# Rows gathered per block through a table made by one-hot matmuls, in place of scatters into slots: attention and mixture of experts on one core

## The reference

```
x = x + xattn(layernorm(x), ctx, ctx, mask, gamma, beta)
x = x + ffn(layernorm(x), w_gate, w_gate_up, w_down)

ffn: gate_probs = softmax(x @ w_gate); only the two highest per token stay, divided by their sum
     gu = einsum('bsd,edh->ebsh', x, w_gate_up);  g, u = split(gu, 2)
     expert_out = einsum('ebsf,efd->ebsd', silu(g) * u, w_down)
     out = einsum('bse,ebsd->bsd', gate_probs, expert_out)
```

## Time and profile before

| what | us |
|---|---|
| device time, median of 3 executions | 491.61 |
| lowest and highest of them | 488.97, 492.09 |
| profiled execution: its span, first to last instruction | 510.0 |
| PE busy in the span | 419.0 (82%) |
| DVE, ACT, POOL busy | 261.6, 201.6, 138.4 |
| TensorE's granted clock, tenths of full speed, in 40 slices of 12.75 us | `9975555575599999999999999999999999999996` |

### The profile page before, as it was taken

The page is one execution under the profiler, slowest core; times in us unless marked ns, Lnnn a source line. Parts: engine busy times, 40 slices in busy tenths (PEclk is TensorE's granted clock), DMA queues, the critical chain, the costliest instruction groups (busy, mean ns, idle before and its releaser), DMA issues.

```text
span 510.0 us, 10031 instructions
## 1 busy us (share of the span) xinstructions
PE 419.0 (82%) x2182; PEld 354.2 (69%) x2183; DVE 261.6 (51%) x601; ACT 201.6 (40%) x358; POOL 138.4 (27%) x122
## 2 busy tenths in 40 slices
PE   4979401060599999999999999999999999999990
PEld 3977201050488888888888888888888888888870
DVE  4786799320355465346556533555555347534330
ACT  2234557000345445345345333454454345423320
POOL 3393582777011211211211112112112112111121
PEclk9975555575599999999999999999999999999996
DMA  8559412642145164134425411354354115212101
GB/s 218 190 142 314 126 62 75 187 154 104 41 118 167 40 163 145 26 78 142 115 72 144 113 31 21 71 134 125 81 144 109 36 21 120 65 21 31 12 11 21
DMA packets 39105, 50.83 MB, mean 100 GB/s; under 512 B 5707, under 2 KB 33971, under 8 KB 39091
## 3 DMA queue, kind: packets, MB, share of 16 engines
q1 hardware_dynamic: 26323, 36.18, 22.9%
q0 software_dynamic: 7152, 9.34, 11.4%
q10 hardware_dynamic: 5616, 5.15, 3.8%
HBM read 33.95 MB, written 16.72 MB: 99 GB/s over the span
## 4 chain that ended last, share of the span: by engine, by line
PE 79%; DVE 6%; another core or an unknown queue 4%; DMA 4%; issue 2%; ACT 1%; POOL 1%; ACTq 1%; SPq 0%; POOLq 0%; DVEq 0%
PE bank L1289 41%; PE bank L1310 14%; PE bank L1312 7%; PE bank L1299 7%; PE bank L1210 3%; PE bank L1274 2%; PE bank L1191 2%; DMA ctx_sb<-in_ctx 1%; DVE act L592 1%; PE bank L1180 1%; DMA slots<-rows,idx 1%; DVE x_sb L648 1%; DVE stats L656 1%; DMA ctxT<-slots 1%
## 5 line engine op out<-in xcount | busy, mean ns | idle before, releaser
L1289 PE MATMUL bank<-w,tokT_hi 128*128 x624 | 173.9, 401 | 21.5 <-DVE tokT_lo L910 20.2
L539 POOL DMA_INDIRECT out<-y_sb,y_idx x39 | 61.4, 1575 | 311.5 <-DVE y_sb L935 300.8
L1289 PEld LDWEIGHTS bank<-w,tokT_hi 128*128 128x128 f32 x624 | 113.6, 191 | 43.9 <-issue 22.4
L919 DVE TENSOR_TENSOR act<-gated,bank 128x512 f32<-128x512 f32 x78 | 53.4, 685 | 137.3 <-ACT gated L1101 137.1
L1310 PE MATMUL bank<-w,aT_hi 128*128 x312 | 119.6, 418 | 0.9 <-DVE y_sb L935 0.9
L1101 ACT ACTIVATE gated<-bank 128x512 f32<-128x512 f32 x78 | 46.7, 598 | 144.7 <-PE bank L1289 133.3
L1289 PE MATMUL bank<-w,tokT_lo 128*128 x312 | 97.5, 394 | 0.0
L1312 PE MATMUL bank<-w,aT_lo 128*128 x312 | 87.7, 281 | 0.0
L1289 PEld LDWEIGHTS bank<-w,tokT_lo 128*128 128x128 f32 x312 | 59.4, 190 | 12.7
L1310 PEld LDWEIGHTS bank<-w,aT_hi 128*128 128x128 f32 x312 | 58.8, 188 | 11.4 <-issue 1.1
L348 DVE TENSOR_TENSOR w<-raw,w x45 | 53.1, 1221 | 22.1 <-ACT w L341 19.2
(11 more groups left out here) (164 smaller groups left out, 311.1 us busy)
## 6 DMA issues: line engine op xcount, KB each, us to landing
raw<-in_L_ffn_w_gate_up SPq DMA_DIRECT2D x32, 512.0 KB
raw<-in_L_ffn_w_down SPq DMA_DIRECT2D x16, 512.0 KB
slots<-empty SPq DMA_DIRECT2D x1, 5031.0 KB, 21.5
ctxT<-slots ACTq DMA_DIRECT2D x39, 129.0 KB
x_sb<-in_x SPq DMA_DIRECT2D x4, 512.0 KB, 6.5
out<-x_sb SPq DMA_DIRECT2D x8, 256.0 KB, 2.2
out<-y_sb,y_idx POOLq DMA_INDIRECT x39, 3.8
ctx_sb<-in_ctx SPq DMA_DIRECT2D x1, 616.0 KB
```

What stands on the lines that cost most here:

```text
L539: pool.indirect_dma_start(out=out, out_offset=bass.IndirectOffsetOnAxis(ap=y_idx[:, s:s + 1], axis=0), in_=y_sb[:, s, :], in_offset=None, ...
L919: dve.tensor_tensor(act[:, h, :], gated[:, h, :], ps_u[h][:, :], ALU.mult).then_inc(act_set, 1)
L1289: ins = pe.matmul(ps[:, :], tokens[:, s, k, :], w.rearrange("p a g d -> p (a g) d"), start=(k == 0 and tokens is tokT_hi and part == 0), s ...
```

## The change

The normalised rows now stay in the order of the tokens in DRAM (`rows_d`, 2048 rows and 128 empty ones); ScalarE's queue writes them, two tiles at a time. Which row a slot needs is worked out on chip: for each of 32 selections (16 tiles, first and second pick) VectorE makes a one-hot matrix of the place in the block (`place_sel`, 128x128) and one of the block (`block_sel`, 128x40). POOL multiplies the latter with the tokens' numbers, and 32 matmuls add up, for each place and block, the number of the token there (`ps_token`). Four VectorE ops make the row's index of it (`row_of`); empty places get spare rows. POOL gathers block b's 128 rows with one indirect DMA (`gather`). The shares go the same way, as a high and a low half, with 32 more matmuls after block 0's products (`turn_shares`), and two VectorE ops (`shares_there`); TensorE and ScalarE wait for them before block 1. The matrices lie in the space of the second expert's weight pieces. The low halves of weight pieces 3 to 5 move from VectorE (L893) to POOL.

```diff
-            pool.wait_ge(att_part, 1)
-            for buf in (rows, x_sb):
-                pool.iota(buf[:, :, D + 1:D + 2].bitcast(I32), pattern=[[P, NT], [0, 1]], base=0,
-                          channel_multiplier=1).then_inc(ids_set, 1)
+            for i in range(RAW, PIECES - 1):
+                split_low(pool, i)
             rsqrt(2, HT, NT, var3, 2, rstd3)
...
+            split_low(pool, PIECES - 1)
+            def at_block(out_sel, value):
+                pool.tensor_tensor(out_sel, block_sel.bitcast(F32), value.unsqueeze(2).to_broadcast([P, SEL, NB2]),
+                                   ALU.mult).then_inc(token_at_set if out_sel is token_at else share_at_set, 1)
+            pool.wait_ge(block_sel_set, 1)
+            at_block(token_at, token_no[:].rearrange("p i n -> p (i n)"))
+            def gather(b):
+                if b >= 2:
+                    pool.wait_ge(tokT_ps, b - 1)
                 pool.indirect_dma_start(
...
+                    out=tok[:, b % 2, :], out_offset=None,
+                    in_=rows_d, in_offset=bass.IndirectOffsetOnAxis(ap=row_of[:, b:b + 1], axis=0)).then_inc(tok_in[b % 2], 16)
...
-            for n in range(NT):
...
-                send(rows, 0, n, first_sent[n * GROUPS // NT])
...
-                send(x_sb, 1, n, last_sent)
+            pool.wait_ge(rows_spare, 16)
+            pool.wait_ge(rows_out, 16 * B)
+            pool.wait_ge(row_of_set, 1)
+            gather(0)
+            gather(1)
+            pool.wait_ge(share_set, 2)
+            at_block(up_at, share_hi[:].bitcast(F32))
+            at_block(low_at, share_lo[:].bitcast(F32))
...
+            gather(2)
+            gather(3)
+            for b in range(NBLK):
+                if b + 4 < NBLK:
+                    gather(b + 4)
+                add(b)
...
@@ vector, behind idx
+            dve.tensor_scalar(slot_of[:], slots, P.bit_length() - 1, None, ALU.arith_shift_right).then_inc(split_index, 1)
+            dve.tensor_scalar(slot_in[:], slots, P - 1, None, ALU.bitwise_and).then_inc(split_index, 1)
...
+            dve.tensor_tensor(block_sel, block_no[:].unsqueeze(1).to_broadcast([P, SEL, NB2]),
+                              slot_of[:].unsqueeze(2).to_broadcast([P, SEL, NB2]), ALU.is_equal).then_inc(block_sel_set, 1)
...
+            for i in range(2):
+                part = slice(i * NT, (i + 1) * NT)
+                dve.tensor_tensor(place_sel[:, part, :], in_block[:].unsqueeze(1).to_broadcast([P, NT, P]),
+                                  slot_in[:, part].unsqueeze(2).to_broadcast([P, NT, P]), ALU.is_equal).then_inc(place_sel_set, 1)
...
@@ vector, behind the shares
+            dve.wait_ge(token_ps, 1)
...
+            dve.tensor_tensor(row_of[:], token_f[:], spare_f[:], ALU.add).then_inc(row_of_set, 1)
...
+            dve.tensor_copy(share_hi[:], shares_f).then_inc(share_set, 1)
...
-            with dve.Fori(RAW, PIECES) as c:
-                split_low(dve, c)
...
@@ scalar
+            def write_rows(b):
+                act_e.wait_ge(rows_set, b + 1)
+                act_e.dma_start(rows_t[:, TPB * b:TPB * (b + 1), :], rows[:, TPB * b:TPB * (b + 1), 0:D]).then_inc(rows_out, 16)
...
             silu(0, 1)
             act_high(0, 0)
-            all_first_sent()
-            load_rows(2, 0)
+            act_e.wait_ge(share_there, 1)
             split_due(act_e, pieces_due(act_e, 0), split_high)
...
@@ tensor
+            pe.wait_ge(token_at_set, 1)
+            for i in range(SEL):
+                if i % NT == 0:
+                    pe.wait_ge(place_sel_set, i // NT + 1)
+                ins = pe.matmul(ps_token, place_sel[:, i, :], token_at[:, i, :], start=(i == 0), stop=(i == SEL - 1))
+            ins.then_inc(token_ps, 1)
+            def turn_shares():
+                pe.wait_ge(share_at_set, 2)
...
+                for i in range(SEL):
+                    ins = pe.matmul(ps_share, place_sel[:, i, :], both_at[:, :, i * NB2:(i + 1) * NB2],
+                                    start=(i == 0), stop=(i == SEL - 1))
...
             turn_tok(1, 1)
             turn_act(0, 0)
+            turn_shares()
+            pe.wait_ge(share_there, 1)
             place = experts(1, 1)
```

More of the change, by code:

```diff
@@ L177, in build, with piece_rows @@
         spent = ctxT[:, :, :, :].rearrange("p b k t -> p (b k t)")
[L178 to L181, removed]
+        tok = spent[:, 0:2 * D].rearrange("p (s c) -> p s c", s=2)
+        y_low = spent[:, 2 * D:3 * D]
+        shares = spent[:, 3 * D:3 * D + 2 * NT * E].rearrange("p (i n e) -> p i n e", i=2, e=E)
+        def piece_rows(c, n):
+            return w2[:, c:c + n].rearrange("p a b g d -> p (a b g d)")
+        place_sel = piece_rows(PIECES, 2).rearrange("p (i c) -> p i c", i=SEL)
+        block_sel, token_at, up_at, low_at = (piece_rows(PIECES + 2 + i, 1)[:, 0:SEL * NB2].rearrange("p (i n) -> p i n", i=SEL)
+                                              for i in range(4))
+        assert 2 * PIECES >= PIECES + 6 and SEL * P == 2 * 2 * PIECE and SEL * NB2 <= 2 * PIECE
         tokT_hi = sb("tokT_hi", [P, 2, KD, P], F32R)
@@ L539, in add @@
                 pool.indirect_dma_start(
[L540 to L548, removed]
+                    out=out, out_offset=bass.IndirectOffsetOnAxis(ap=row_of[:, b:b + 1], axis=0),
@@ L550, in _ @@
+                    in_=y_sb[:, b % 2, :], in_offset=None, compute_op=ALU.add).then_inc(added, 16)
+            gather(2)
[4 more added lines that the diff above has]
+                add(b)
+            pool.wait_ge(added, 16 * NBLK)
         @block.vector
@@ L1058, in _ @@
                 slot_rows(b)
+                write_rows(b - 1)
+            write_rows(B - 1)
             act_e.activation(inv_sq[:, 0:1], inv_sq[:, 0:1], ACT.Silu)
             act_e.wait_ge(tables_set, 1)
[L1063 to L1090 removed]
             def tok_high(b, s):
@@ L1114, in low_result, with experts @@
                     act_e.wait_ge(y_set, b)
-                act_e.activation(y_low, ps_y[:, D:2 * D], ACT.Copy, scale=at(keys, b)[:, 0:1].bitcast(F32)).then_inc(y_low_set, 1)
-            def experts(b, s, loads=1, late=False, last=False):
+                act_e.activation(y_low, ps_y[:, D:2 * D], ACT.Copy, scale=one(share_at, b)).then_inc(y_low_set, 1)
+            def experts(b, s, last=False):
                 silu(b, 0)
@@ L1145, in _ @@
             act_high(0, 0)
-            all_first_sent()
-            load_rows(2, 0)
+            act_e.wait_ge(share_there, 1)
             split_due(act_e, pieces_due(act_e, 0), split_high)
-            experts(1, 1, loads=0, late=True)
-            experts(2, 0, loads=2)
-            with act_e.Fori(1, NBLK // 2 - 2) as i:
+            experts(1, 1)
+            experts(2, 0)
+            with act_e.Fori(1, NBLK // 2 - 1) as i:
                 experts(2 * i + 1, 1)
                 experts(2 * i + 2, 0)
-            experts(NBLK - 4, 1)
-            for b in range(NBLK - 3, NBLK):
-                experts(b, b % 2, loads=0, last=b == NBLK - 1)
+            experts(NBLK - 2, 1)
+            experts(NBLK - 1, 0, last=True)
             act_high(NBLK - 1, 1)
```

194 lines of the change are left out of this document (85 added, 109 removed).

## The result

The changed kernel takes 508.42 us (507.63 to 509.66, 4 executions) where the kernel before takes 490.34 (488.97 to 492.09, 4): ratio 1.036, interval 1.033 to 1.039, so 18.1 us slower. The forecast was 500.4, in 491 to 507: the direction holds, the size doesn't, and the time lies above the range. The profiled execution of the changed kernel took 509.05, its span is 507.1. A second profile of the kernel before (**before_again**, taken beside the experiments) took 491.17, span 489.2, and has no gap of 20 us: it is the one to compare with, and the difference of both spans is 17.9.

A forecast was written before the change was run, and what follows sets the result against it. From 143 us on TensorE was taken as the bound, so only that stretch's start and what lies between blocks could move. Terms 5.3 (block 0) + 3.5 (turning the shares) = 8.8; 491.6 + 8.8 = 500.4 us, range 491 to 507.

The forecast's parts named there:

- The ids, +7.2: Ahead of the rows' table: VectorE waits for POOL's moved splits, so the ids come at 90.7, not 83.5 us.
- first two pieces: Behind the first reciprocal root: VectorE's residual and product wait for two POOL splits, +4.8 us, bounds 0 and 5.
- Token matmuls, 0.16 each: Ahead of the rows' table: TensorE's 32 small products take 0.16 us each, the last 16 ending at 103.0.
- I take it that they slip through: 0: Before block 0: VectorE's last table ops escape POOL's share products, 0; if not, 1.7 or 5 us.
- rival A: Before block 0: POOL's share products catch the tables, +1.7 to +5, giving 502 to 505.4 us; chance 0.28.
- The sum to block 0: From the ids to block 0's rows: rows there at 108.3 us against 103.0, so +5.3.
- Turning the shares, +3.5: Behind block 0's products: 32 products, 2.9 us, then TensorE waits 0.6 for VectorE's two small ops.
- The second 16 scatters: 0 to 1 us: Beside blocks 0 to 2: removing these scatters, met at block 4's load, gains 0 to 1 us.
- In the blocks: 0: In the block loop: POOL's gathers ahead of each add delay nothing, 0 us.
- The gap: Before block 1 in the profile of before: 20.53 us without a named releaser, taken as belonging to that execution only.
- rival C: The scatters cause the gap and timed executions hold part of it: 488.4 with 12 us, 480 with all; chance 0.12.
- Rivals B and D: B: moved splits matter little, +1.6, 493.2 us, chance 0.15. D: gathers late in the loop, 78 us, chance 0.03.

The follow-up runs named there:

- a1: The changed kernel with the low halves of pieces 3 to 5 back on VectorE, while it waits for the token matmuls: 501.44 us, ratio 1.019.
- a4: The changed kernel with the edits of a1, a2 and a3 together: 495.66 us, ratio 1.011.
- a2: The changed kernel, but POOL makes its products for the shares only when the tables are set: 503.04 us, ratio 1.025.
- b1: The kernel before, with the low halves of pieces 3 to 5 made on POOL: 494.9 us, ratio 1.0076.
- a3: The changed kernel with TensorE's three table reads for block 1 ahead of its wait for the shares: 504.27 us, ratio 1.027.
- a6: The changed kernel without the 32 share matmuls and VectorE's sum of them, every share set to 1: 506.08 us, ratio 1.030.
- a8: a4 with 32 bytes of padding ahead of the weight buffers, nothing else: 494.19 us, ratio 1.007.
- a10: a7 with the pairs written behind gather 0's landing, share gathers and VectorE's share op later, and tiles at a8's addresses: 483.81 us, ratio 0.954.
- a7: The changed kernel with shares gathered from DRAM as pairs, token_at's product and low halves on VectorE, places made in four parts: 489.33 us, ratio 0.995.

## Why the prediction was wrong in size and right in direction

- **The ids, +7.2: right.** They are ready at 89.9, 6.4 later than the earlier trace rows and 6.7 later than in before_again, by the waits forecast in the places forecast. Of "first two pieces", +4.8, the residual ends at 78.2 and L803 at 80.6, 4.3 later than the 76.3 of before; the third adds the rest at L841, 2.1. The Trainium skill ("SBUF — State Buffer", "Who interferes with whom") was cited for this; the trace agrees: these two-input ops take 2.4 to 2.8 beside POOL's splits.
- **Token matmuls, 0.16 each: too low.** They take 0.22 (7.03 for 32), at a granted clock of 0.50. The forecast's own scaling, 0.28 x 168/256, gives 0.18 and not 0.16. The first begins only when token_at is there, at 96.05, since POOL's product waited 2 us for VectorE. The table of rows comes at 103.86 all the same, against 103.8: the place matrices were done at 98.2 and not at 100.4, and the errors cancel.
- **"I take it that they slip through: 0": this step failed.** TensorE waited 5.1 us for the tables; rival A is what happened, at its upper end. The gather was not slow (median 3.3, below my 4.0); VectorE's op was caught ahead of POOL's first product and waited for the second as well. The forecast had priced the meeting at 1.7 or 5 and then took 0 on the strength of half a microsecond, and a1 beside a4 shows that an op recorded half a microsecond ahead of the product is caught all the same. a2, which removes only this meeting, brings block 0's products forward by 4.25 and gives 5.3 back. Who is let through differs: between the two splits (75.30, x2) VectorE got its residual done and POOL waited, between the two share products none of VectorE's ops. In the changed kernel the op that waited, L930, has a single input, and the forecast had looked only at ops with two. The same section of the Trainium skill counts copies and tensor_scalar among the ops that can take the shared port, where their operands meet its conditions; by that rule, this trace agrees (5.32 us).
- **The sum to block 0: +5.3 forecast, +9.7 found against the earlier trace rows, +11.3 against before_again.** The profile of before that the sum was made from has block 0's products at 104.90, 1.6 later than before_again: its transfers were 1.0 slower (5.47 and 4.47 against 5.07 and 3.86), its ids 0.3 later. This is the second piece of the miss.
- **Turning the shares, +3.5: mis-sized; the stretch grew by 6.4.** Of this 5.0 lies between the end of block 0's products and block 1's (6.26 against 1.31): the matmuls, 3.52 where 2.9 were expected, VectorE's ops, 0.5 for 0.6, and 1.0 not counted, TensorE's reads of its tables, which now stood behind the share wait (`127.78 1.63 issue`), where before they lie in a pause of 0.65. The other 1.45 is block 0's products, 8.56 instead of 7.11 because the clock rose 6.0 into them and not 3.0. They lie ahead of the turn, and take 7.1 to 8.6 in the profiles here, the kernel before with b1's edit included (8.61). Block 1's first products, 5.27 instead of 3.01, come on top, in the next stretch. a3 shows the reads (1.5); a6 shows that without the matmuls the clock falls all the same.
- **"The second 16 scatters: 0 to 1 us": too low, a gain that was missed.** before_again loses about 4 us between blocks 1 and 4 to the scatter that lands in 3.73. The changed kernel gets them back, but gives 2.2 of it up at half clock (30.62 where a4 takes 28.45). a4 keeps 3.8.
- **"In the blocks: 0": it was 1.8.** A block is 0.056 us longer, over the 34.5 blocks of the table's last stretch. Not from the gathers, for which the forecast had argued, but from where the buffers lie (a8).
- **The gap: right for the comparison, open as a cause.** The forecast took the 20.53 of the earlier trace rows as that execution's own. before_again has none, and the sum by differences holds. But on the chip of the last run every execution of the kernel before took 12 to 21 us more than 491.5, six of the eleven with spans of 509.3 to 510.8 and a mean granted clock of 0.893 to 0.897, like the 510.0 and 0.894 of the first profile, while a10, which has no scatters, took what the other chips' numbers let expect. So rival C (the gap is the scatters' doing) isn't dead: it would hold where the gap comes each time. There is no profile of before from that chip, and no timing of the changed kernel beside such executions.
- **Rivals B and D** fell: the port costs what it was priced at, no gather is late in the loop (PE 30.59 of 30.60 us busy).

Summed up: 18.1 measured against 8.8 forecast leaves 9.3. Block 0's products stood at 104.90 + 5.3 = 110.2 in the forecast and came at 114.59, which is 4.4, the tables' 5.1 less small terms that were too dear; 1.6 is block 0's later start in the profile of before; 2.9 the turn (6.4 for 3.5); 1.8 the buffers' place; less 1.7 for the scatters' wait. That is 9.0.

## What to carry to other kernels

When two engines share a port, look at every place where they can meet, not at the one that the change moves, and take a meeting within half a microsecond as happening. A new wait on TensorE costs its length and the register reads behind it, and in five of the eight profiles with this wait the clock fell about it too; move the reads ahead of it. Compare the ends as well: a kernel can gain where nobody changed anything. A new tile shifts all behind it: compare the steady part before blaming the new work, and send small scattered data after the transfer that something waits for.

## What the runs showed that I had not expected

- One VectorE instruction on one partition and 39 elements took 5.32 us because of two POOL instructions of 2.35 in a row, and it was recorded 0.62 ahead of the first.
- A write of 16 KB in pieces of 8 bytes took 8.1 us to land, and the gather of 128 KB issued 3.8 later took 8.0 instead of a median of 3.3. In a10, with the write moved behind it, the gather was there within 3.6 (issued 97.98, rows turned at 101.56). The rival, the raw pieces, was there in both: SP issued the first at 95.14 in a7, at 95.52 in a10 and at 95.59 in a4, the second at 105.26, 99.56 and 99.71. From 96 to 102 the core's transfers moved 36 GB/s in a7, 158 in a10 and 137 in a4, so with the pairs ahead of them all transfers were slow, and the raw pieces alone don't do it.
- POOL's closing DRAIN took 5.87, 6.43 or 1.8 us, by the kernel, 4.6 us of a kernel's time that no forecast here had as a term.
- 32 bytes of padding changed each block from 9.442 to 9.396 us. The value was the same to 0.001 in all seven kernels with the same addresses.
- The kernel before took 491.5 us on three chips and 511.3 (503.3 to 512.5) on a fourth.
